# Decoding spread over the steps, the FFN's turns one step apart, and the attention jobs in a new order on up to four banks

## What is computed

```python
x = x + tanh(g_xattn) * sigmoid(xn @ wg.T) * (attention(xn, ctx) @ wo.T)   # 16 heads of 32, xn = rmsnorm(layernorm(x)) * norm_w
gate, up = split(layernorm(x) @ w_gu)            # 512 -> 2 x 1408, weights in 4 bits with a scale for each 128 inputs
y = (silu(gate) * up) @ w_down.T                 # 1408 -> 512, 4 bits with scales
x = x + tanh(g_ffn) * y / rms(y)
```

## Time and profile before

| | |
|---|---|
| median of 3 runs | 725.06 us (722.46 to 725.78) |
| the profiled execution | 723.83 us, of it 722.0 us span |
| loop bodies | three of 96.0 us, about 90 to 378 us |
| last attention steps, last outputs, start of the FFN | about 378 to 430 us |
| FFN | about 423 to 722 us |
| granted TensorE clock, mean | 0.898 |
| busy | TensorE 83%, VectorE 67%, ScalarE 45%, GpSimd 32% of the span |

### The profile page before, as it was taken

The page is one execution under the profiler, slowest core; times in us unless marked ns, Lnnn a source line. Parts: engine busy times, 40 slices in busy tenths (PEclk is TensorE's granted clock), DMA queues, the critical chain, the costliest instruction groups (busy, mean ns, idle before and its releaser), DMA issues.

```text
span 722.0 us, 12496 instructions
## 1 busy us (share of the span) xinstructions
PE 601.8 (83%) x4154; PEld 528.8 (73%) x4154; DVE 480.4 (67%) x1062; ACT 323.3 (45%) x865; POOL 227.6 (32%) x242
## 2 busy tenths in 40 slices
PE   1699957899858899488997777699699799699997
PEld 1598847888658787488885556587598697599984
DVE  6745795556975569855645349689689679677741
ACT  2754332433325433334343215375465465376630
POOL 5710130000310002100000006487476476477740
PEclk9988976899969999569998599799999999899999
DMA  8440154012451032410286430100100010000011
GB/s 270 144 136 3 46 190 164 1 47 89 156 189 52 24 101 97 160 58 0 68 312 209 180 105 1 65 1 1 65 28 7 26 68 30 30 1 30 30 58 45
DMA packets 26842, 59.36 MB, mean 82 GB/s; under 512 B 3625, under 2 KB 3753, under 8 KB 26793
## 3 DMA queue, kind: packets, MB, share of 16 engines
q1 hardware_dynamic: 26792, 58.76, 24.0%
HBM read 39.62 MB, written 19.14 MB: 81 GB/s over the span
## 4 chain that ended last, share of the span: by engine, by line
PE 50%; DVE 24%; ACT 8%; issue 8%; POOL 7%; DMA 2%; DVEq 0%; SPq 0%; ACTq 0%; POOLq 0%
PE bank L257 19%; PE bank L1526 13%; PE bank L1539 10%; PE bank L1377 3%; ACT probs L719 3%; DVE nmax L937 2%; PE bank L1353 2%; DVE xn L932 2%; POOL hT_lo L629 2%; DVE pT_lo L942 2%; DVE part_gate L1221 1%; DVE vb_lo L905 1%; DVE part_up L1221 1%; DMA xb<-x_scratch 1%; DVE words L1040 1%
## 5 line engine op out<-in xcount | busy, mean ns | idle before, releaser
L1526 PE MATMUL bank<-mT_hi,wgu 128*128 128x320 f32 x440 | 142.2, 333 | 13.9 <-ACT part_up L838 5.4
L1526 PE MATMUL bank<-mT_lo,wgu 128*128 128x320 f32 x440 | 137.9, 323 | 0.0
L719 ACT ACTIVATE probs<-bank,nmax 100x96 f32<-100x96 f32 x256 | 66.1, 342 | 157.3 <-DVE nmax L937 157.3
L1526 PEld LDWEIGHTS bank<-mT_hi,wgu 128*128 128x128 f32 x440 | 88.4, 201 | 25.6 <-ACT part_up L838 7.5
L1526 PEld LDWEIGHTS bank<-mT_lo,wgu 128*128 128x128 f32 x440 | 88.6, 201 | 3.6
L636 POOL TENSOR_TENSOR part_gate<-part_gate 128x320 f32<-128x320 f32 x55 | 57.1, 1039 | 92.8 <-DVE part_gate L1221 92.8
L838 ACT ACTIVATE part_up<-bank,scale 128x320 f32<-128x320 f32 x110 | 57.4, 522 | 56.2 <-PE bank L1526 56.1
L566 POOL TENSOR_TENSOR rstd<-var,halfpow 100x1 f32<-100x1 f32 x16 | 13.7, 857 | 210.4 <-DVE var L927 210.4
L838 ACT ACTIVATE part_gate<-bank,scale 128x320 f32<-128x320 f32 x110 | 52.4, 525 | 61.7 <-PE bank L1526 42.8
L1221 DVE SCALAR_TENSOR_TENSOR part_gate<-bank,scale,part_gate 128x320 f32<-128x320 f32 x110 | 55.8, 545 | 30.1 <-ACT part_gate L838 18.2
L1221 DVE SCALAR_TENSOR_TENSOR part_up<-bank,scale,part_up 128x320 f32<-128x320 f32 x110 | 58.3, 546 | 24.5 <-ACT part_up L838 17.7
(11 more groups left out here) (130 smaller groups left out, 1573.2 us busy)
## 6 DMA issues: line engine op xcount, KB each, us to landing
gate_up_scratch<-left SPq DMA_DIRECT2D x12, 512.0 KB, 5.5
down_scratch<-left SPq DMA_DIRECT2D x12, 512.0 KB, 2.9
wgu<-gate_up_scratch SPq DMA_DIRECT2D x11, 512.0 KB, 7.0
words<-in_packed SPq DMA_DIRECT2D x18, 256.0 KB
xn<-in_x SPq DMA_DIRECT2D x16, 200.0 KB
xa<-in_x SPq DMA_DIRECT2D x16, 200.0 KB
x_scratch<-gate SPq DMA_DIRECT2D x16, 200.0 KB
ctx_raw<-in_ctx_tail SPq DMA_DIRECT2D x4, 768.0 KB, 9.6
```

Source lines behind the costliest of these rows:

```text
L719: last = nc.scalar.activation(probs[i % 2][:, cols], SC[i % HPG][0:L, cols], ACT.Exp, bias=nmax[:, i % 4, b:b + 1])
L1526: last = nc.tensor.matmul(product_bank(j, t, i, k)[:, 0:TG], wgu[t][:, k, 128 * i:128 * i + 128], mT[j % 2][half][:, k, :], start=half == ...
```

## The change

Four things are changed together.

1. **Decoding**: 26 stages, two a step, from step 6 to step 2 of the next group, all behind the row maxima (`DECODE_AT`). SP's queue follows the same order, with loads and stores placed at their steps (`cycle`).
2. **Order of the jobs**: X0 to X3 go to steps 8 to 11, one each, K0 to 11, T2 and A0 to 13, A1 to 14, A2 alone to 15, Q0 alone to 12, G1 moves up to 7. `NORM_AT` puts two statistics each in steps 6 and 7, `CTX_AT` the context in steps 9 and 10.
3. **Banks**: each job has a bank by table (`BANK_OF`), 0, 1, and 2 and 3 while the scores don't hold them. `before_in_bank` finds the last user, the scores among them; the scores wait for each bank by itself.
4. **FFN**: `TURN_AT` 5, 6, 7 becomes 5, 7, 9; `ROUND` is rotated so that the first products meet the banks of the last outputs one by one.

```diff
-        ROUND, TURNED = (2, 3, 4, 5, 0), bank[1]
-        TURN_AT = (5, 6, 7)
+        ROUND, TURNED = (5, 2, 0, 3, 4), bank[1]
+        TURN_AT = (5, 7, 9)
...
-        BESIDE = {0: ["Q1", "B0"], 1: ["K1", "T3", "B1"], 2: ["O0"], 3: ["O1", "B2"], 4: ["Q2", "O2"], 5: ["O3", "K2", "T0"],
-                  6: ["G0"], 7: ["Q3"], 8: ["K3", "G1"], 9: ["T1", "G2"], 10: ["G3"], 11: ["X0", "X1"], 12: ["X2", "X3", "Q0"],
-                  13: ["K0", "T2"], 14: ["A0"], 15: ["A1", "A2"]}
-        NORM_AT = {6: 0, 7: 1, 8: 2, 9: 3}
-        CTX_AT = {9: (0, 1), 10: (2,), 11: (3,)}
-        PIECE_AT = {8 + q: q for q in range(len(KINDS))}
+        BESIDE = {0: ["Q1", "B0"], 1: ["K1", "T3", "B1"], 2: ["O0"], 3: ["O1", "B2"], 4: ["Q2", "O2"], 5: ["O3", "K2", "T0"],
+                  6: ["G0"], 7: ["Q3", "G1"], 8: ["K3", "X0"], 9: ["T1", "G2", "X1"], 10: ["G3", "X2"], 11: ["X3", "K0"],
+                  12: ["Q0"], 13: ["T2", "A0"], 14: ["A1"], 15: ["A2"]}
+        NORM_AT = {6: (0, 1), 7: (2, 3)}
+        CTX_AT = {9: (0, 1), 10: (2, 3)}
+        STAGES = [(q, stage) for q in range(len(KINDS)) for stage in range(5 if KINDS[q] == "d" else 4)]
+        DECODE_AT = {((LOOP_FROM + n // 2) % STEPS, 1): STAGES[n:n + 2] for n in range(0, len(STAGES), 2)}
+        BANK_OF = dict(G0=0, Q3=2, G1=1, K3=0, X0=3, T1=2, G2=1, X1=0, G3=1, X2=0, X3=2, K0=1, Q0=0, T2=2, A0=1, A1=0, A2=2,
+                       Q1=1, B0=3, K1=0, T3=2, B1=3, O0=1, O1=0, B2=2, Q2=1, O2=0, O3=1, K2=0, T0=1)
+        BANK_OF_LAST = {**BANK_OF, **dict(O0=0, O1=1, O2=3, O3=4)}
...
+            def cycle(g, last=False):
+                pieces_before(g)
+                for i in range(LOOP_FROM, LOOP_FROM + STEPS):
+                    i %= STEPS
+                    for place in range(3):
+                        for unit in DECODE_AT.get((i, place), ()):
+                            behind_decoding(g, *unit)
+                    for name in BESIDE[i]:
+                        if name[0] == "X" and not last:
+                            load_tokens(g + 1, int(name[1]))
+                        elif name[0] == "O":
+                            output(g, int(name[1]))
+                    if i == CONTEXT_AT and not last:
+                        load_context(g + 1)
...
                 probsT_lo(g, i)
                 dequant(0)
                 if not isinstance(g, int) or g or i:
                     attn_norm(*last_step(g, i))
-                dequant(1)
                 for ahead in step_ahead(g, i):
                     row_max(*ahead)
-                dequant(2)
-                if not last and i in NORM_AT:
-                    layer_stats(g + 1, NORM_AT[i])
+                dequant(1)
+                if not last:
+                    for b in NORM_AT.get(i, ()):
+                        layer_stats(g + 1, b)
...
-                if not isinstance(n, int) or n:
-                    pe.wait_ge(s_exp, n)
                 for h in range(HPG):
+                    open_bank(g + 1 if f"S{hg}" in OF_LAST else g, f"S{hg}", 2 + h)
                     nc.tensor.matmul(SC[h][0:L, 0:KC], ones[HD * h:HD * h + 1, :], mb[HD * h:HD * h + 1, :], start=True, stop=False)
```

More of the change, by code:

```diff
@@ L277, in build @@
+        USERS = IN_STEPS[IN_STEPS.index("X0"):] + IN_STEPS[:IN_STEPS.index("X0")]
+        OF_LAST = [n for n in USERS if n[0] in "GTO" and n not in IN_STEPS[:IN_STEPS.index("X0")] and n != "T0"]
+        OF_LAST += [n for n in ("S2", "S3") if n not in IN_STEPS[:IN_STEPS.index("X0")]]
+        CYCLE = [n for n in USERS if n[0] != "S"]
+        SPLIT_JOBS = [n for n in CYCLE if n[0] in "XQKABT"]
+        NORM_AT = {6: (0, 1), 7: (2, 3)}
+        CTX_AT = {9: (0, 1), 10: (2, 3)}
         MASK_AT = 11
-        AHEAD = 2
@@ L279, in build @@
-        SCORES_AT = 2
-        PIECE_AT = {8 + q: q for q in range(len(KINDS))}
+        STAGES = [(q, stage) for q in range(len(KINDS)) for stage in range(5 if KINDS[q] == "d" else 4)]
+        DECODE_AT = {((LOOP_FROM + n // 2) % STEPS, 1): STAGES[n:n + 2] for n in range(0, len(STAGES), 2)}
+        CONTEXT_AT = 13
         STATS_AT, TURNED_AT = 12, {13: 0, 14: 1, 15: 2}
-        FIRST_CYCLE = [n for n in CYCLE if n not in OF_LAST]
+        FIRST_CYCLE = HEAD + [n for n in CYCLE if n not in OF_LAST and n not in HEAD]
@@ L387, in load_next, with output @@
                 load_tail_mask(g + 1)
-            def outputs(g, last):
+            def load_next(g):
                 for b in range(NB):
[L391 to L397, removed]
+                    load_tokens(g, b)
+                load_context(g)
+            def output(g, b, last=False):
+                sp.wait_ge(s_x1, NB * g + b + 1)
+                sp.dma_start(x1_dram[bass.ds(NB * g + b, 1)].rearrange("o t d -> (o t) d"), gate[b][:, :])\
+                  .then_inc(s_x1st[b], 16)
+                if b + 2 < NB:
+                    load_residual(g, b + 2)
+                elif not last:
+                    load_residual(g + 1, b - 2)
             def load_piece(g, q):
@@ L475, in _ @@
                     pieces_before(g)
-                    for q in range(len(KINDS)):
-                        next_piece(g, q)
+                    for unit in STAGES:
+                        behind_decoding(g, *unit)
                 all_kept()
@@ L489, in _ @@
                 with sp.Fori(0, GROUPS - 2) as g:
[L490 to L500, removed]
+                    cycle(g)
+                cycle(GROUPS - 2, True)
                 all_kept()
@@ L514, in _ @@
                 load_down()
-                outputs(GROUPS - 1, True)
+                for b in range(NB):
+                    output(GROUPS - 1, b, True)
                 for b in range(NB):
@@ L964, in output, with step, dequant @@
                                                ALU.mult, ALU.add).then_inc(s_x1, 1)
-            def step(g, i, last=False):
-                def dequant(stage):
-                    if not last and i in PIECE_AT:
-                        decode(g, PIECE_AT[i], stage)
+            def step(g, i, last=False, cycle=None):
+                def dequant(place):
+                    if cycle is not None:
+                        for q, stage in DECODE_AT.get((i, place), ()):
+                            decode(cycle, q, stage)
                 probsT_lo(g, i)
@@ L989, in step @@
                         job_lo(c, name)
-                if not last and i - 1 in NORM_AT:
-                    normalise(g + 1, NORM_AT[i - 1])
-                dequant(4)
+                if not last:
+                    for b in NORM_AT.get(i - 1, ()):
+                        normalise(g + 1, b)
+                dequant(2)
                 if last and i == STATS_AT:
@@ L1286, in _, with open_bank @@
         def _(pe):
[L1287 to L1288 removed]
+            def open_bank(c, name, number):
+                before = before_in_bank(c, name, number)
                 if before is None:
@@ L1522, in products @@
                     open_bank_of(FT * j + t, KT * i + k)
-                    if j == 0 and t == 0 and KT * i + k == len(ROUND) - 1:
-                        pe.wait_ge(s_gated, NB * GROUPS)
+                    if j == 0 and t == 0:
+                        for b in range(NB):
+                            if product_bank(j, t, i, k) is job_bank(GROUPS, f"O{b}"):
+                                pe.wait_ge(s_gated, NB * (GROUPS - 1) + b + 1)
                     for half in (HI, LO):
```

101 lines of the change are left out of this document (55 added, 46 removed).

## The result

The kernel after takes 671.24 us (median of four runs, 669.12 to 673.15), the one before, run beside it, 723.76: ratio 0.927, 95% interval 0.923 to 0.931. The profiled execution took 673.15 us with a span of 671.3, so it is the longest of the four. The forecast was 682 us.

A forecast was written before the change was run, and what follows sets the result against it. It took TensorE's waits for VectorE's lo copies, plus lower clock, as the bound. From 723.8 us, less 17.7 (loop) and 25 (FFN turns), came 681.1; runs' median 1.3 above: 682, own range 672 to 692, overall 660 to 706.

The forecast's parts named there:

- the hole before Q0: Loop body: TensorE's largest gap, 5.4 us waiting for X3's lo copy, claimed to be gone after the change.
- The bodies: Three loop bodies: from 96.0 us each to 90.9, 90.9 and 88.5, a gain of 17.7 us.
- The two other bodies last as long.: Kernel before: one loop body was read at 96.0 us and the two others taken to last the same.
- The waits: Loop body after: TensorE's remaining or new stops, summed to 11.8 us, or 9.4 without the late first piece.
- the late piece: Step 6, two bodies of three: first load lands 6.5 us after the store; VectorE stands 2.5, TensorE waits 0.9 and 1.1.
- Clock: Loop bodies after: 5 us lost per body to low-clock stretches, against 7.2 before.
- FFN turns: Transposes of the next group's tiles: eight waits for the lo copy, 24.2 us, vanish, plus 1 for clock: 25; bounds 12, 32.
- The rest: Head, last ten steps and weight loads: no change, all zero within 1 us.
- The loop gives nothing: Rival: VectorE's new leads and the late piece cancel the loop's gain; body 96, time 700 us; chance 0.18.
- turns give half: Rival: FFN turns gain only 12 us, the loop its 18; time 695 us; chance 0.08.
- The clock takes the loop's gain: Rival: short stops hold TensorE at the lower clock, 16 us more; body 98, time 706 us; chance 0.08.
- more than forecast: Rival: loop waits halved and no clock loss, a loop gain of 42 us; time 658 us; chance 0.08.

The follow-up runs named there:

- order_only: Kernel after, but with a whole decoded piece in each of steps 8 to 13 again: 694.17 us, ratio 0.962 to the kernel before.
- spread_only: Kernel before with new FFN turns, spread decoding and SyncE's new queue, jobs in old order on two banks: 672.84 us, ratio 0.932.
- early_words: Kernel after, with the next body's first two pieces and first scales loaded as soon as their buffers are free: 665.24 us, ratio 0.920.
- attention_only: Kernel after with the old FFN turns at 5, 6, 7: 697.29 us, ratio 0.965 to the kernel before.
- turns_only: Kernel before with only the FFN turns moved to 5, 7, 9: 698.24 us, ratio 0.968.
- head_banks: Kernel after with the jobs of the head and the first group's steps 0 and 1 on banks 0 and 1: 670.46 us, ratio 0.927.
- all_three: Kernel after with early_words, ctx_early and head_banks together: 662.4 us, ratio 0.918 to the kernel before.
- words_ctx: Kernel after with early_words and ctx_early together: 661.83 us, ratio 0.916 to the kernel before.
- behind_jobs: Kernel after, with the decode stages of steps 1, 9 and 13 moved behind the jobs' copies: 674.83 us, ratio 0.933.
- the square: Four kernels, all with new FFN turns: neither other part 698.2 us, order and banks alone 694.2, spreading alone 672.8, both (after) 671.2.
- ctx_early: Kernel after, with the context halves cast one step earlier, at steps 8 and 9: 669.24 us, ratio 0.925.

## Why the prediction was right, and where it was not

The mechanism it named for the FFN is what the runs show. For the loop it did not part the spreading from the order. It says that the hole before Q0 is gone because "between X3 and Q0 now lie K0 and a whole step base"; but order_only has that order too and stops 4.9 us before the scores of step 10 instead, while spread_only keeps the old order, has 2.8 us at Q0 and nearly the whole gain.

**The bodies, 17.7 us predicted, 31.6 measured.** Both sides of the subtraction were off. In PE's three parts, before: idle 44.1 (295.44 less 251.29), loss to the clock 27.8 (half of the 55.6 us that it worked in 78.5 us of low stretches), own 223.5, or 74.5 a body. After: idle 21.5, clock 17.0, own 225.4, or 75.1. The first of the eight low stretches of before, and their sum:
```profile
70.20:73.60 3.40, 3.40 (x12) 2.38 (x9) 1.50 (x4) 1.03 (x4) 0.57 (x1) 0.50 0.02 5
...
sum 78.50, PE 55.58 PEld 50.65 DVE 45.04 ACT 25.78 POOL 12.06; mean PE 6.95 PEld 6.33 DVE 5.63 ACT 3.22 POOL 1.51
```

- *"The two other bodies last as long."* This step failed: they last 101.2 and 98.3, with 4.5 and 2.9 us more busy time at clock 0.85 and 0.86 for 0.89. 7.4 us of the miss. It could be read in the trace of before, as three windows.
- *The waits, 11.8 and 9.4 us*, were 8.5, 7.9 and 5.1: 33.0 predicted, 21.5 measured. (By its own terms the sum without the late piece is 9.8, not 9.4.) All but those of steps 0 and 1 were where they were named:

| place | predicted | measured, second body |
|---|---|---|
| X0 at step 8 and the transposes after it (late piece) | 0.9 + 1.1 | 1.92 + 0.36 |
| scores, step 10 | 2.3 | 1.76 |
| K0, step 11 | 1.7 | 1.78 |
| scores, step 14 | 1.25 | 0.72 |
| steps 0 and 1 | 0.7 + 1.2 | none over 0.3 |
| scores, step 2 | 2.6 | 1.21 + 0.48 |

  The waits behind DVE's lead were all sized too large, and K0's was right. The late piece's two waits came out at 2.3 us for 2.0, but the piece itself was mis-sized: it lands 8 us behind the store and not 6.5, DVE stands 4.4 us and not 2.5, and it also lengthens the scores' wait of step 10 by 0.9 (early_words).
- *Clock, 5 us a body*: 5.7 measured (17.0 in three), on a PE of 75.1 us of its own and not 74.1. Both together 5.1 us more in three bodies.

In the sum the waits are 11.5 us less than predicted, PE's other time 5.1 more, and the bodies of before 7.4 more: 11.5 - 5.1 + 7.4 = 13.8 us of gain on top, against 13.9 measured (31.6 less 17.7). Of what was to show it, the first body fell out of 88 to 92, below; the two others, the stops of DVE at the head of two bodies, K0's wait and the groups of 48 to 52 us came as written.

**FFN turns, 25 predicted, 23.9 measured, with a wrong split.** Idle in the four groups fell by 18.4 us (38.2 to 19.8) and not 24.2: waits of 0.4 to 1.1 us for `part_up` and `part_gate` came in the steps around the turns, as the bounds allowed. From tanh 5 to tanh 8 it counted 13.2 us for DVE, and 14.0 were measured. But busy time fell by 5.5, not 1, since clock 0.97, 0.97 and 0.94 became 1.00. That the eight waits are what the change removes is shown by attention_only, that nothing else of it matters there by turns_only.

**The rest, 0 predicted, +4.8 measured.** The error is the start. In the first 66.35 us PE did less (43.9 us busy before, 40.3 after) at a lower clock:
```profile
0.00:66.35 66.35, 43.85 (x333) 40.42 (x333) 40.57 (x83) 32.54 (x83) 26.23 (x32) 0.92 0.45 150
```
before, and after
```profile
0.00:66.35 66.35, 40.27 (x302) 37.54 (x303) 41.57 (x78) 31.92 (x81) 26.66 (x32) 0.86 0.45 150
```
Scores of the first group wait for a K and a B copy in their banks (0.5 and 0.6 us), and from 57.5 to 67.7 us PE works at the low level (clock 0.50), where before has a clock of 0.88 in the same window. head_banks takes the banks back, has neither these waits nor this stretch, and starts 5.3 us earlier. That shows where the two waits come from. It does not show that the banks make the stretch: all_three has the same banks in the head and no such waits, and still works at 0.50 from 56.2 to 66.4 us and starts at 69.7, as words_ctx does at 69.6; behind_jobs has the banks of after and only 3.4 us at the low level there (58.1 to 61.5), and starts at 68.0. The start is 4.6 us late for a reason that stays open in the main. Taking the banks back does not help either: in head_banks the first body waits 1.3 for K2's copy at its first scores and works at clock 0.90 in place of 0.92.

**The rivals.** *The loop gives nothing* and *turns give half* are out by the square and by turns_only. *The clock takes the loop's gain* is out as stated: clock 0.92 to 0.94 in the bodies, against 0.85 to 0.89. (Its 44 us of PE work for steps 6 to 2 do not fit the prediction's own list either, which has 56 there; by that the rival would have been dearer still.) A small form of it is true, and it decides what the order is worth: in after each of the nine low stretches begins 0.9 to 2.1 us after PE came out of a stop (eight times before scores, once K0's in the first body), PE works through all of them, and against spread_only 5.0 of the 9.3 us of idle time saved are lost so. The Trainium skill describes the like (TensorE: Matmul & The Clock Gate, A second HAM failure mode: psum-queue depth-cycling): short idles between groups of matmuls let the clock go back and forth, at a cost in throughput between the bursts. The trace agrees on the direction, at 5.7 us a body where the rival had 16 (and the kernel before 9.3). The result lies between the forecast and *more than forecast* (658), nearer to the forecast. No luck hides in the number: the errors of the three terms, 13.9 us of gain more, 1.1 less and 4.8 less, leave 8.0 us of the 50.7.

What stays open: why one stop is followed by a low stretch and another (K0's 1.8 us in the second and third body, X0's 1.9) is not, and with it why ctx_early runs between 665 and 673 us, while words_ctx stays within 2.

## What to carry to other kernels

Spread foreign work evenly over the steps before touching the order of the jobs: here the square gives 25 us to the one and 4 or less to the other, and a cleverer order costs waits of its own (banks shared with the scores, a context wanted two steps sooner, a first load that is suddenly late). When work moves to the head of a loop body, move its load to where its buffer comes free in the body before; and a copy that one engine makes at the end of a step and another wants at the start of the next belongs one step further off. Read all passes of a loop, not one, and split each into idle time, work at the low clock and own work before subtracting.

## What the runs showed of the hardware that was not expected

The same normalisation of VectorE lasts 0.54 us or 2.2, by what GpSimd does beside it. Before:
```profile
189.59 2.22 DVE L932 TENSOR_SCALAR xn<-xn,mv,rstd 100x512 f32<-100x512 f32 x1
196.18 0.54 DVE L932 TENSOR_SCALAR xn<-xn,mv,rstd 100x512 f32<-100x512 f32 x1
```
The first runs beside the context's lo halves on GpSimd, the second beside nothing:
```profile
189.57 1.96 POOL L561 TENSOR_TENSOR ctxT_lo<-ctx_raw,ctxT_hi 128x384 fp32r<-128x384 f32 x2
```
After, all twelve stand clear of GpSimd and take 542 ns in the mean, 963 before; in words_ctx, which puts the casts back beside them, 855. A body's DVE time fell from 66.2 to 64.0 us, 1.7 of it by this one normalisation, with the same instructions.

And the same code of a loop body lasts from 95.8 to 101.2 us (before and turns_only, six bodies) by where its low stretches fall: idle time runs from 14.0 to 15.6 us, PE's busy time from 81.3 to 85.8.
